# Query, key and value bias added on TensorE, last tiles cleared on ScalarE, and ten fewer zero products

## What is computed

```python
x = x + _L0_attn_ref(_layernorm(x), Wq, bq, Wkv, bkv)   # the bias is used here
x = x + _L0_ffn_ref(_layernorm(x), ...)                 # 2 experts, top 1
x = x + _L1_attn_ref(_layernorm(x), ...)                # state-space scan
x = x + _L1_ffn_ref(_layernorm(x), ...)                 # 64 experts, top 6, capacity 64, plus a shared one

# inside _L0_attn_ref
q = (x @ Wq.T + bq).reshape(b, l, h, hd)                # 16 heads of 16
kv = (x @ Wkv.T + bkv).reshape(b, l, 2, hd)
k, v = kv[:, :, 0], kv[:, :, 1]
attn = softmax(einsum('blhd,bld->blh', q, k)[..., None] / sqrt(hd), axis=-1)
out = (attn * v[:, :, None, :]).reshape(b, l, -1)
```

## Time and profile before

| | |
|---|---|
| median of 3 runs | 651.9 us (650.84 to 652.97) |
| the profiled execution | 651.51 us, of which the span of its instructions is 649.8 us |
| busy in the span | PE 565.8, DVE 519.9, ACT 191.4, POOL 134.2 us |
| mean granted PE clock | 0.929 of full speed |
| chain that ended last | DVE 41%, PE 30%, DMA 11%, issue 5%, ACT 4% |

### The profile page before, as it was taken

One profiled execution on the slowest core, in us unless ns is written; L12 is line 12 of the kernel. 1 busy time (PEld: TensorE's weight loads), 2 busy tenths in 40 slices (PEclk: granted clock), 3 DMA queues, 4 the chain that ended last, 5 costly groups with the idle time before them and its releaser, 6 DMA issues.

```text
span 649.8 us, 7620 instructions
## 1 busy us (share of the span) xinstructions
PE 565.8 (87%) x2418; PEld 353.2 (54%) x2418; DVE 519.9 (80%) x1195; ACT 191.4 (29%) x372; POOL 134.2 (21%) x129
## 2 busy tenths in 40 slices
PE   7467999799999969999899866759889999989898
PEld 6344666444667446674456643428475444433387
DVE  6998888354899969999999999999998466458727
ACT  2113312225443254432544304422111322322100
POOL 2120201220001200002000120000000667678650
PEclk9679999987999959999899967689999999999899
DMA  7961000327301184001730207938472599995475
GB/s 281 411 202 36 33 1 34 113 66 260 130 0 44 31 289 175 0 34 33 261 130 1 75 31 261 346 118 285 157 242 68 171 352 345 351 328 97 57 267 169
DMA packets 62741, 102.06 MB, mean 157 GB/s; under 512 B 6999, under 2 KB 52823, under 8 KB 62192
## 3 DMA queue, kind: packets, MB, share of 16 engines
q1 hardware_dynamic: 50640, 81.78, 35.9%
q0 software_dynamic: 9760, 17.71, 10.7%
q10 hardware_dynamic: 2304, 2.10, 1.0%
HBM read 79.80 MB, written 25.46 MB: 162 GB/s over the span
## 4 chain that ended last, share of the span: by engine, by line
DVE 41%; PE 30%; DMA 11%; issue 5%; ACT 4%; POOL 2%; DVEq 0%; ACTq 0%; SPq 0%
DVE scan_area L1404 10%; DMA part_rows<-bc,att_s 9%; PE gate_ps L768 6%; PE up_ps L768 5%; DVE scan_area L1407 5%; DVE scan_area L1400 5%; PE misc_ps L785 4%; DVE sig L1344 2%; PE turn_ps L701 2%; DMA front_area<-sorted_dram 1%; DVE work L1494 1%; DVE bc L1558 1%; PE turn_ps L957 1%; DVE front_area L1349 1%; DVE ln_st L1157 1%
## 5 line engine op out<-in xcount | busy, mean ns | idle before, releaser
L1404 DVE TENSOR_TENSOR_SCAN scan_area<-scan_area 128x1024 f32<-128x1024 f32 x32 | 73.3, 2292 | 3.9 <-ACT scan_area L1078 0.5
L768 PE MATMUL gate_ps<-big,front_area 128*128 x144 | 72.8, 631 | 1.4 <-ACT front_area L978 1.4
L785 PE MATMUL misc_ps<-big,front_area 128*128 x288 | 67.5, 388 | 2.4 <-ACT front_area L978 2.4
L768 PE MATMUL up_ps<-big,front_area 128*128 x144 | 68.4, 597 | 0.0
L785 PEld LDWEIGHTS misc_ps<-big,front_area 128*128 128x128 f32 x288 | 55.0, 194 | 14.1 <-issue 6.7
L1014 ACT ACTIVATE sig<-gate_ps 128x512 f32<-128x512 f32 (+1 forms) x48 | 28.6, 596 | 111.9 <-PE up_ps L768 80.1
L677 POOL DMA_INDIRECT part_rows<-bc,att_s x32 | 50.4, 1575 | 23.4 <-DMA part_rows<-bc,att_s 14.5
L1344 DVE SCALAR_TENSOR_TENSOR sig<-sig,gate_ps 128x512 f32<-128x512 f32 (+1 forms) x48 | 32.8, 683 | 23.9 <-ACT sig L1014 23.6
L1078 ACT ACTIVATE scan_area<-scan_area,a_col 128x511 f32<-128x511 f32 x64 | 41.9, 714 | 29.7 <-DVE scan_area L1404 26.2
L648 POOL DMA_INDIRECT front_area<-ysorted_dram,slot_idx x16 | 20.2, 1264 | 138.2 <-DMA ysorted_dram<-front_area 134.6
L768 PEld LDWEIGHTS up_ps<-big,front_area 128*128 128x128 f32 x144 | 28.1, 195 | 36.2 <-issue 36.2
(11 more groups left out here) (290 smaller groups left out, 1000.5 us busy)
## 6 DMA issues: line engine op xcount, KB each, us to landing
bc<-bc_dram SPq DMA_DIRECT2D x4, 4096.0 KB, 13.7
big<-in_wgu SPq DMA_DIRECT2D x14, 704.0 KB, 8.9
part_rows<-zeros SPq DMA_DIRECT2D x16, 512.0 KB, 15.3
front_area<-in_wgu SPq DMA_DIRECT2D x6, 704.0 KB, 7.8
scan_area<-in_wgu SPq DMA_DIRECT2D x6, 704.0 KB, 9.3
big<-in_wd SPq DMA_DIRECT2D x12, 256.0 KB, 7.8
table<-row_area SPq DMA_DIRECT2D x4, 640.0 KB, 4.2
x_res<-in_x SPq DMA_DIRECT2D x4, 512.0 KB, 8.0
```

The lines of the kernel that those rows point to most:

```text
L768: mm = pe.matmul(bank[:], xs_t[:, k, j, :], gu0[:, expert_of[b, j], k, g, half * 512:(half + 1) * 512], start=(k == 0), stop=(k == K - 1))
L785: mm = pe.matmul(misc_ps[:, 0:D], h0_t[:, half, c * P:(c + 1) * P], dn0[:, expert_of[b, j], half * 4 + c, :], start=(half == 0 and c == 0) ...
L1404: nc.vector.tensor_tensor_scan(buf.rearrange(flat), d_a[:, g % 2, :, :].rearrange(flat), buf.rearrange(flat), 0.0, ALU.mult, ALU.add).then ...
```

## The change

Four things are edited.

1. The bias is one more PE product for each tile: `ones[0:1, :]` (one row of 128 ones) by the bias row (1x288), into the same accumulation as the other two. DVE's addition at L1208 goes, and the counts of `attn_steps` (`AT_DIFF`, `AT`) go down by one.
2. The bias is loaded to one partition only. The wait for `w_attn_loaded` stands on PE, ahead of the first `attn_qkv`, instead of on DVE.
3. The eight clears of `parts[8]` to `parts[15]` are ACT copies of broadcast zeros, behind ACT's other work of the same pair, instead of DVE memsets. The count of `down1_filled` that they wait for is one lower.
4. `WAKE_LAST` is 10 instead of 20.

```diff
--- before.py
+++ after.py
@@ -63,7 +63,7 @@
 TABLE_ROWS = N + P
 PART_ROWS = PER_TOKEN * N + E * EMPTY_STEP
 YO_RING = 4
-WAKE_LAST = 20
+WAKE_LAST = 10
 TILES = B * J
 LATE = TILES // 2
 BY_PE = [0, 2, 4, 6, 8, 9, 10, 11, 12]
@@ -76,7 +76,7 @@
 
 ROOT = 9
 LN = 3 * J + ROOT
-AT_DIFF, AT = 5, 10
+AT_DIFF, AT = 4, 9
 RT_SEL, RT_DIFF = J + 1, J + 2
 RT_OPS = [J + 11, J + 17, J + 23, J + 27]
 RT_AT = [sum(RT_OPS[0:b]) for b in range(B + 1)]
@@ -490,8 +490,8 @@
             sp.dma_start(x_res[:, 0:J, :], xv[:, 0:J, :]).then_inc(x_loaded[0], 16)
             sp.dma_start(w_qkv[:, :, 0:D], wq_t.rearrange("(k p) n -> p k n", p=P)).then_inc(w_qkv_loaded, 16)
             sp.dma_start(w_qkv[:, :, D:QKV], wkv_t.rearrange("(k p) n -> p k n", p=P)).then_inc(w_qkv_loaded, 16)
-            sp.dma_start(b_qkv[:, 0:D], row(bq, D)).then_inc(w_attn_loaded, 16)
-            sp.dma_start(b_qkv[:, D:QKV], row(bkv, 2 * HD)).then_inc(w_attn_loaded, 16)
+            sp.dma_start(b_qkv[0:1, 0:D], bq.rearrange("(o n) -> o n", o=1)).then_inc(w_attn_loaded, 16)
+            sp.dma_start(b_qkv[0:1, D:QKV], bkv.rearrange("(o n) -> o n", o=1)).then_inc(w_attn_loaded, 16)
             sp.dma_start(g0_row[:].rearrange("p e d -> p (e d)"),
                          row(gate0.rearrange("e d -> (e d)"), 2 * D)).then_inc(w_attn_loaded, 16)
             for b in range(1, B):
@@ -735,11 +735,13 @@
                 slot, use = turn.next()
                 if b == 0 and j == 0:
                     pe.wait_ge(w_qkv_loaded, 16 * 2)
+                    pe.wait_ge(w_attn_loaded, 16 * 3)
                 pe.wait_ge(turn_moved, use - 1)
                 for k in range(K):
-                    mm = pe.matmul(turn_ps[slot][:, 0:QKV], xn_attn_t[:, k, j, :], w_qkv[:, k, :],
-                                   start=(k == 0), stop=(k == K - 1))
-                mm.then_inc(turn_filled, 1)
+                    pe.matmul(turn_ps[slot][:, 0:QKV], xn_attn_t[:, k, j, :], w_qkv[:, k, :],
+                              start=(k == 0), stop=False)
+                pe.matmul(turn_ps[slot][:, 0:QKV], ones[0:1, :], b_qkv[0:1, :], start=False, stop=True
+                          ).then_inc(turn_filled, 1)
 
             def route_slots(b, _):
 
@@ -1131,6 +1133,10 @@
                     move_rows(p + 1)
                 if p >= 1:
                     move_h1(p - 1)
+                if CLEAR_FROM <= p < CLEAR_FROM + LATE:
+                    act.wait_ge(down1_filled, CLEAR_FROM - 2)
+                    nc.scalar.copy(parts[LATE + p - CLEAR_FROM].rearrange("p (r d) -> p r d", r=PER_TOKEN),
+                                   zeros[:, 0:D].unsqueeze(1).broadcast_to([P, PER_TOKEN, D])).then_inc(late_clear, 1)
 
             move_rows(0)
             run_pairs(pair)
@@ -1203,31 +1209,27 @@
                 dve.wait_ge(qkv_copied, b + 1)
                 q4 = qkv[:, :, 0:D].rearrange("p j (h d) -> p j h d", h=H)
                 k4 = qkv[:, :, D:D + HD].unsqueeze(2).broadcast_to([P, J, H, HD])
-                if b == 0:
-                    dve.wait_ge(w_attn_loaded, 16 * 3)
-                tt(qkv, qkv, b_qkv[:].unsqueeze(1).broadcast_to([P, J, QKV]), ALU.add).then_inc(attn_steps, 1)
+                tt(w4, q4, k4, ALU.mult).then_inc(attn_steps, 1)
                 dve.wait_ge(attn_steps, b * AT + 1)
-                tt(w4, q4, k4, ALU.mult).then_inc(attn_steps, 1)
+                reduce(score, mix.rearrange("p j (h d) -> p (j h) d", h=H), AX, ALU.add).then_inc(attn_steps, 1)
                 dve.wait_ge(attn_steps, b * AT + 2)
-                reduce(score, mix.rearrange("p j (h d) -> p (j h) d", h=H), AX, ALU.add).then_inc(attn_steps, 1)
+
+                reduce(best, score.unsqueeze(2), AX, ALU.max).then_inc(attn_steps, 1)
                 dve.wait_ge(attn_steps, b * AT + 3)
-
-                reduce(best, score.unsqueeze(2), AX, ALU.max).then_inc(attn_steps, 1)
-                dve.wait_ge(attn_steps, b * AT + 4)
                 tt(diff, score, best, ALU.subtract).then_inc(attn_steps, 1)
 
             def attn_add(b, _):
                 v4 = qkv[:, :, D + HD:QKV].unsqueeze(2).broadcast_to([P, J, H, HD])
                 dve.wait_ge(attn_exp, b + 1)
                 reduce(den, ex.unsqueeze(2), AX, ALU.add).then_inc(attn_steps, 1)
+                dve.wait_ge(attn_steps, b * AT + 5)
+                recip(rec, den).then_inc(attn_steps, 1)
                 dve.wait_ge(attn_steps, b * AT + 6)
-                recip(rec, den).then_inc(attn_steps, 1)
+                tt(prob, ex, rec, ALU.mult).then_inc(attn_steps, 1)
                 dve.wait_ge(attn_steps, b * AT + 7)
-                tt(prob, ex, rec, ALU.mult).then_inc(attn_steps, 1)
-                dve.wait_ge(attn_steps, b * AT + 8)
                 tt(w4, v4, prob.rearrange("p (j h) -> p j h", j=J).unsqueeze(3).broadcast_to([P, J, H, HD]),
                    ALU.mult).then_inc(attn_steps, 1)
-                dve.wait_ge(attn_steps, b * AT + 9)
+                dve.wait_ge(attn_steps, b * AT + 8)
                 xb = x_res[:, bass.ds(b * J, J), :]
                 tt(xb, xb, mix, ALU.add).then_inc(attn_steps, 1)
                 wait_apart(dve, passed["dve"], (attn_steps, (b + 1) * AT))
@@ -1591,9 +1593,6 @@
                         ).then_inc(reach_steps, 1)
                     dve.wait_ge(reach_steps, 6)
                     ts(late_idx, late, float(N), None, ALU.add).then_inc(reach_steps, 1)
-                if CLEAR_FROM <= p < CLEAR_FROM + LATE:
-                    dve.wait_ge(down1_filled, CLEAR_FROM - 1)
-                    nc.vector.memset(parts[LATE + p - CLEAR_FROM], 0.0).then_inc(late_clear, 1)
 
             run_pairs(pair)
             for p in (PAIRS - 2, PAIRS - 1):
```

## The result

The changed kernel takes 665.45 us (median; 663.44 to 667.35) against 651.9: ratio 1.0191 with an interval of 1.015 to 1.0233. That is slower, by 1.5 to 2.3%, and outside the range of the prediction. The profiled execution took 667.35 us, 665.6 of it the span.

What follows compares the result with a forecast made beforehand. PE, not DVE, was taken to set the pace of the front's full stretch. From 651.5 us, the front's +3.0 and the end's -2.1 gave 652.4 us, with a range of 648.4 to 655.6.

Steps and rivals of the forecast that it cites:

- Bias, the price of one product: Front, PE: each one-row bias product costs 0.485 us, like a deep one; nine of sixteen lie where PE decides.
- the front's upper end: Worst case up to 102 us: +1.3 us if the clock rises where it did, +2.4 for five later products, +3.7.
- The other steps of the front: Bias up to 102 us: +0.6 us to the first routing, +2.4 for five products in PE's full stretch, +3.0.
- The first routing's product: Front, after batch 1: DVE's 1.35 us saved, four bias products add 1.94 us, so routing comes +0.6 us later.
- The moved wait for the gate weights: Front, PE's first query product: weights land at 9.8 us against a start at 12.66, so it costs nothing.
- Clears on ACT: Last pairs: each clear takes about 1.15 us, hidden in ACT's 2.18 us wait; PE's 1.60 us wait for DVE goes.
- From put 23 to put 31: Last puts: without DVE's clears the last put stands about 1.1 us nearer to pair 23's.
- The end: Last put to finish, ten zero products fewer: -1.0 us if puts gain nothing, -2.1 with the puts' -1.1.
- The stores: End: three more finished tiles stored before part 6 is in delay its landing by 1.0 us.
- That PE's full stretch has room: Faster rival, 51.95 to 101.86 us: added products slip into PE's stream, DVE sets the pace; 648.0 us, chance 0.2.
- The clock's fall between the loads: Slower rival, end: PE's idling between part loads brings 6.8 us at half clock behind part 6; 655.8 us, chance 0.15.
- That the end gives nothing: Rival, end: puts no earlier, stores delay part 6 by 2 us, the front's +3.0 stands alone; 654.5 us, chance 0.15.

Runs made afterwards that it cites:

- e5: The changed kernel with the bias product 128 rows deep (identity by bias rows on all partitions): 652.7 against 653.3 us, ratio 1.0021.
- e3: The kernel before with the bias as a 128-deep PE product, clears still on DVE and 20 zero products: 654.07 against 650.88 us, 1.0048.
- e9: The kernel before with only the eight clears moved to ACT, 20 zero products: 650.05 against 649.75 us, 1.0006.
- e2: The kernel before with clears on ACT and 10 zero products, bias as before: 649.35 against 650.88 us, 0.9985.
- e4: The kernel before with its 20 zero products at the end one row deep: 659.09 against 650.88 us, measured once.
- e10: The kernel before with every second of its 20 zero products one row deep: 662.48 against 648.65 us, measured once.
- e7_thin_b3: e3 with the one-row bias product in batch 3 only: 658.73 against 653.3 us for the kernel before, 1.0067.
- e7_thin_b2: e3 with the one-row bias product in batch 2 only: 663.07 against 653.3 us for the kernel before, 1.0152.
- e1: The changed kernel with clears on DVE and 20 zero products, so the one-row bias alone: 664.1 against 650.88 us, 1.0192.

## Why the prediction was wrong

**The step that failed** is the first one of "Bias, the price of one product": "The nearest rows say that depth saves nothing". For a product by itself that is so. The Trainium skill says the same ("TensorE: Matmul & The Clock Gate", section "Why this matters for your kernels"): a single product of 32 rows takes the time of one of 128. Rows 5 also had a hint to look closer: the median of the 32-deep records is 692 ns, and 592 of the 128-deep ones. Each of those 32-deep products stands behind a wait of PE (0.67 and 0.78 us for the first two); its first record takes 692 ns at full clock, its second 587. None of them ran directly behind a deep product, so the row could not show what that costs. But I took 0.485 from that with no bound above it; measured it is 0.88. What I asked of the rows was how long a thin product takes. The question was what it does between two deep ones. A nearer row was there. The chain of the kernel before has, in a pair at full clock, a 96-deep product (L929) behind 128-deep ones (L928):

```profile
512.57 0.58 PE ssm_ps L928 x4
513.15 0.64 PE ssm_ps L929 x2
```

0.64 us for one product of 256 columns, where a zero product of 256 columns takes 8.63 / 20 = 0.43. L928 also fills 64 columns of the array and not 128, so the row doesn't separate the two changes; as a bound it would have done: 0.485 + 2 x 0.2 = 0.9 us.

**What it is worth.** Without the clock, 0.4 us more for each of the nine products that count are 3.6 us: 656.0, already above the range. The clock has the rest, and here a second step failed: the front's upper end, +3.7, let the low clock cost 0.7 us more than before. PE worked at the low clock for 7.6 us before, for 32.6 us after and for 9.5 us in e5 (10.2 us low), and half of the difference is work lost: 12.5 us against before, 11.5 against e5. Batch 3's norm is 12.0 us later than in e5. The two causes sum to more than that, up to 11.5 + 16 x 0.4 = 17.9, since part of each falls into PE's waits; only for batches 2 and 3 were they taken apart.

**The other steps of the front** fit once the product is deep. Batch 3's norm is 2.7 us later in e3 and 3.8 in e5, forecast +3.0, with the 1.8 us of spread above. The first routing's product starts at 38.30 in e3 and at 37.64 before: +0.66, forecast +0.6. That closeness is luck, as this product starts between 37.0 and 38.9 in the traces with an unchanged front. The moved wait for the gate weights cost nothing: the first query product starts at 12.73 (12.66 before).

**Clears on ACT:** 1.05 us each, forecast 1.15, and hidden. PE's wait of 1.60 us and the low clock behind it are gone: 632.00 to 638.00 has clock 1.00. From put 23 to put 31 it is 18.38 us instead of 19.24, -0.9, forecast -1.1. But the trace of before is at the slow end here: the ten kernels with clears on DVE have 18.29 to 19.24 us, 18.8 in the mean, the four with clears on ACT 18.29 to 18.40. The gain is nearer to 0.4 than to 1.1, in line with e9.

**The end:** from the last put to the end 30.3 us instead of 31.8, -1.5, forecast -1.0. In all -2.4 in the profiled execution, forecast -2.1. Over the traces with 20 deep zero products this stretch is 30.2 to 32.1 us, over the four with 10 it is 30.1 to 30.5, 1.1 less in the mean. The stores cost part 6 less than 1.0 us: it lands 17.0 us after the last put, 16.8 before. Six sums took 10.6, forecast 10.4.

**The rivals.** That PE's full stretch has room fell: it wanted batch 3's norm earlier than before, and with the deep products it is 2.7 and 3.8 us later. With it falls, for this kernel, the rule of the Trainium skill cited beside it ("Perfetto Trace Analysis", section "Identifying the Most-Contended Engine"), by which weight loads at 60% leave headroom. The clock's fall between the loads came, 3.4 us long from 642.8, but ahead of part 6, where it was free, as the text allowed. That the end gives nothing can't be excluded by times (e2 [0.9966, 1.0003]); part 6's landing and the six sums speak against it. I had put the danger of the clock at waits; it lay in the products that I added.

## What to carry to other kernels

Price an added product by its neighbours in the queue: read the distance of starts across a change of depth, and not the duration of a like product by itself. For a bias, copy the row to all partitions and use the identity, or leave it on the engine that has it, which was 3 us better here; a product that looks small can cost more than a full one. Where PE comes out of a wait at the low clock, put only full-depth products behind it.

## What the runs showed that I had not expected

- A change of depth between neighbouring f32 products costs 0.20 us at full clock, each time, for 1, 32 and 64 rows against 128, and 0.29 at half clock (1.15 instead of 0.86, one row).
- The granted clock fell to 0.50 with PE busy for the whole of the stretch: from 623.9 in e4 and from 628.4 in e10, and never in those 8.6 us when all zero products were 128 deep:

```profile
623.00:631.60 8.60, 8.60 (x41) 7.56 (x41) 2.23 (x4) 0.00 (x0) 6.70 (x7) 1.00 0.99 381
```

The Trainium skill ties a fall to waits of TensorE ("TensorE: Matmul & The Clock Gate", section "HAM oscillation — how this bites in real kernels"). Here there was none, and the measurement decides. What it is about shallow or mixed products that the clock answers to stays open.
- In the third pair of the last layer ACT starts its tanh some 1.9 us late in the changed kernel, e5, e7_thin_b3 and e7_thin_b2, with no work shown that it waits for, and not in the kernel before, e1, e2 and e3 (the trace puts the wait down to "remote", 3.53 us). In the changed kernel PE then ran at 0.50 from 526.8 to 533.6, and its first put came 3.1 us after e1's. That is more than its end gives back, so the changed kernel is no faster than e1, and whole times of these four kernels hold a cost that is not the bias. Its cause was not looked for; the verdict on the bias rests on e1, e3 and batch 3's norm, which are free of it.
